# VectorE makes the first sum of two blocks by heads, GpSimd two more steps of each unit, and work at the end of the attention moves ahead of the last stage

## The reference

```
h = layernorm(x) * (1 + ca) + sa
c_kv = h @ W_kv_down;  k = c_kv @ W_k_up;  v = c_kv @ W_v_up;  q = h @ W_q         # 16 heads of 32
q_rope, k_rope = rotary(h @ W_q_rope), rotary(c_kv @ W_k_rope)                      # 32 columns, one for all heads
scores = (q k^T + q_rope k_rope^T) / 8, causal;  w = softmax(scores)
x = x + ga * ((w @ v) @ W_o)
h = layernorm(x) * (1 + cb) + sb
xr, xk = mixes of h with h one token earlier (mu_r, mu_k)
x = x + gb * sigmoid(xr @ W_r^T) * (relu(xk @ W_k^T)^2 @ W_v^T)
```

## Time and profile before

| | |
|---|---|
| time, median of 3 runs | 3523.52 us (3522.85 to 3524.01) |
| the profiled execution | 3526.95 us |
| its span, first to last instruction | 3524.8 us |
| granted TensorE clock, mean | 0.994 |
| PE busy | 3450.0 us, 98% |
| POOL busy | 2799.4 us, 79% |
| DVE busy | 2556.9 us, 73% |
| ACT busy | 1802.9 us, 51% |

### The profile page before, as it was taken

The page is one execution under the profiler, slowest core; times in us unless marked ns, Lnnn a source line. Parts: engine busy times, 40 slices in busy tenths (PEclk is TensorE's granted clock), DMA queues, the critical chain, the costliest instruction groups (busy, mean ns, idle before and its releaser), DMA issues. The chain is left out here.

```text
span 3524.8 us, 53405 instructions
## 1 busy us (share of the span) xinstructions
PE 3450.0 (98%) x19088; PEld 2395.2 (68%) x19088; DVE 2556.9 (73%) x5361; ACT 1802.9 (51%) x3423; POOL 2799.4 (79%) x1252
## 2 busy tenths in 40 slices
PE   8999989999999999999999999999999799999999
PEld 4777756666666666666666666666665588888887
DVE  6777777787877878778778787787775466666665
ACT  2333335556556565565555655656556444344343
POOL 2333359999999999999999999999999566666665
PEclk9999999999999999999999999999999899999999
DMA  5789763463544635526346354363461221111120
GB/s 208 272 285 320 263 165 84 106 152 72 128 106 96 145 80 117 135 70 153 87 111 145 78 124 112 87 155 80 108 154 48 75 72 65 68 68 64 72 72 36
DMA packets 232753, 426.52 MB, mean 121 GB/s; under 512 B 25380, under 2 KB 26916, under 8 KB 232488
## 3 DMA queue, kind: packets, MB, share of 16 engines
q1 hardware_dynamic: 232424, 423.10, 44.6%
q10 hardware_dynamic: 64, 0.02, 0.0%
HBM read 300.86 MB, written 121.65 MB: 120 GB/s over the span
## 5 line engine op out<-in xcount | busy, mean ns | idle before, releaser
L1170 POOL TENSOR_TENSOR att_sum_g<-att_sum_g,att_probs 128x2048 f32<-128x2048 f32 (+3 forms) x458 | 1757.5, 3837 | 53.8 <-ACT att_probs L1070 3.8
L1070 ACT ACTIVATE att_probs<-att_ps_s 128x512 f32<-128x512 f32 (+3 forms) x2560 | 1309.6, 535 | 924.3 <-PE att_ps_s L1231 828.1
L1106 DVE TENSOR_REDUCE att_piece_max<-att_ps_m 128x1 f32<-128x512 f32 x1520 | 964.1, 681 | 242.7 <-PE att_ps_m L1214 240.4
L1230 PE MATMUL att_ps_s<-att_q_a,att_k_a 128*128 128x512 f32 (+3 forms) x2560 | 946.1, 374 | 9.8 <-DMA att_k_b<-s_kr_hi 8.3
L1231 PE MATMUL att_ps_s<-att_q_b,att_k_b 65*128 65x512 f32 (+3 forms) x2560 | 931.3, 368 | 0.0
L1109 DVE CUSTOM_DVE_ANT_0 att_ps_m<-att_ps_m,mask_qk 128x128 f32<-128x128 f32 x1008 | 478.3, 511 | 238.4 <-PE att_ps_m L1214 218.8
L1214 PE MATMUL att_ps_m<-att_k_a,att_q_a 128*128 128x512 f32 (+3 forms) x1808 | 644.1, 380 | 1.5 <-DVE att_piece_max L1106 1.0
L1230 PEld LDWEIGHTS att_ps_s<-att_q_a,att_k_a 128*128 128x128 f32 x2560 | 485.5, 190 | 116.2 <-issue 25.7
L1237 PE MATMUL att_ps_o<-att_probs,att_v 128*32 128x512 f32 (+3 forms) x5120 | 540.1, 534 | 0.0
L1231 PEld LDWEIGHTS att_ps_s<-att_q_b,att_k_b 65*128 65x128 f32 x2560 | 484.0, 189 | 64.9
L1214 PEld LDWEIGHTS att_ps_m<-att_k_a,att_q_a 128*128 128x128 f32 x1808 | 340.1, 190 | 236.9 <-DVE att_piece_max L1106 89.7
(11 more groups left out here) (190 smaller groups left out, 4888.2 us busy)
## 6 DMA issues: line engine op xcount, KB each, us to landing
att_q_a<-s_q_hi SPq DMA_DIRECT2D x128, 256.0 KB, 6.1
att_q_a<-s_qr_hi SPq DMA_DIRECT2D x128, 256.0 KB, 6.8
prj_x_sb<-in_x_dram SPq DMA_DIRECT2D x16, 1024.0 KB, 5.8
s_q_hi<-prj_q_hi SPq DMA_DIRECT2D x16, 1024.0 KB, 4.2
s_q_lo<-prj_q_lo SPq DMA_DIRECT2D x16, 1024.0 KB, 5.4
s_k_hi<-prj_k_hi SPq DMA_DIRECT2D x16, 1024.0 KB, 4.6
s_k_lo<-prj_k_lo SPq DMA_DIRECT2D x16, 1024.0 KB, 7.1
s_v<-prj_v_sb SPq DMA_DIRECT2D x16, 1024.0 KB, 9.0
```

Of the source, the lines that this page charges most:

```text
L1070: act.activation(probs[t % RING][:, hh, c0:CH], ps_s[(GH * t + hh) % SBANKS][:, c0:CH], ACT.Exp, scale=SCALE).then_inc(probs_ready, 1)
L1106: dve.tensor_reduce(top, ps_m[:, bank, :], AX_X, ALU.max).then_inc(piece_taken, 1)
L1170: pool.tensor_tensor(sum_g[:, :, c0:CH], sum_g[:, :, c0:CH], new, ALU.add).then_inc(sum_added, 1)
L1230: mm(out[:, c0:CH], k_a[:, hh, i * P:(i + 1) * P], q_a[j][:, hh, c0:CH], start=True, stop=False)
```

## The change

Five edits in one diff:

1. `SHARE_OF` gives the full steps 8 of block 2 and 6 of block 3 (steps 20 and 30 of a unit) to POOL in place of PE. Block 3 now has no "T" but in the last unit (`SHARE_LAST` is as it was), so whether a block's `ps_d` is opened by the sum is asked for each unit and block.
2. For blocks 2 and 3 DVE makes the first sum, step 0 + step 1, into `sum_g`: four additions of 128x512, one for each head (`open_sum`), in its list for t = FIRST[j] + 3, between parts of that step's maxima. POOL's first add of such a block is now the third step's, and waits for all four (`sum_opened`). ACT waits for `sum_opened` where it reuses the two buffers that DVE reads.
3. `CLOSE_LATER` of block 3 becomes 2 (in the last unit the closing stays at the last t).
4. `deal` counts `OPENING` = 11 in the pairs of steps where DVE opens a sum, and with `CLOSE_LATER` the pair that holds block 3's closing is the one after.
5. The seam: ACT's splits of `w_o` and of the first attention block, DVE's and POOL's low halves of them, PE's turning of `w_r` and ACT's copy of it stand at the end of the attention's lists; the tensors lie over attention buffers no longer in use. SP doesn't wait for the last store at the end of the attention; before it issues that store it waits for all earlier ones, and the last stage waits for it ahead of the load of the second attention block. The first output product waits for all low halves at once.

```diff
-SHARE_OF = ("GGGG", "GGGGGGGG", "GGGGGGGGTGGT", "GGGGGGTGGGGGGGGG")
+SHARE_OF = ("GGGG", "GGGGGGGG", "GGGGGGGGGGGT", "GGGGGGGGGGGGGGGG")
+OPENED_BY_VECTOR = (2, 3)
...
-CLOSE_LATER = (0, 2, 2, 0)
+CLOSE_LATER = (0, 2, 2, 2)
 CLOSES_FIRST = [owners[-1] == "T" and not later for owners, later in zip(SHARE_OF, CLOSE_LATER)]
-OPENED_BY_SUM = ["T" not in (owners.rstrip("T") if first else owners) for owners, first in zip(SHARE_OF, CLOSES_FIRST)]
...
+def opened_by_sum(u, j):
+
+    owners = owners_of(u, j)
+    return "T" not in (owners.rstrip("T") if CLOSES_FIRST[j] else owners)
...
+            if j in OPENED_BY_VECTOR and n < 2:
+                continue
             if n:
...
-PIECE, CLOSING = 2.8, 19
+PIECE, CLOSING, OPENING = 2.8, 19, 11
 
 
 def deal(items, pairs, late, early):
 
-    closes = lambda m: CLOSING * any((FIRST[j] + STEPS[j] + 2 + CLOSE_LATER[j]) % NSTEP == 2 * m for j in range(TCH))
+    closes = lambda m: CLOSING * any((FIRST[j] + STEPS[j] + 2 + CLOSE_LATER[j]) % NSTEP == 2 * m for j in range(TCH)) + \
+        OPENING * any(FIRST[j] + 2 == 2 * m for j in OPENED_BY_VECTOR)
...
+def last_stage_views(nc):
+
+    with ExitStack() as ctx:
+        sb = lambda n, s, d: ctx.enter_context(nc.sbuf_tensor("ffn_" + n, s, d))
+        sb("under_att", [P, 2 * GH * CH + GH * T], F32)
+        att = sb("att_hi", [P, NG, CH], F32R), sb("att_lo", [P, NG, CH], F32R)
+        return att, ctx.enter_context(nc.psum_tensor("ffn_ps_t2", [P, NC, CH], F32))
+
+
+def output_weight(ops):
+
+    return [ops["k_a"][:, part, :].rearrange("p (c n) -> p c n", c=NC) for part in (0, 1)]
...
+        def opened(u, j):
+
+            return GH * (len(OPENED_BY_VECTOR) * u + OPENED_BY_VECTOR.index(j) + 1)
...
-        CLOSE_AT = {t + CLOSE_LATER[j]: (u, j) for t, (u, j) in TAKE_AT.items()}
+        CLOSE_AT = {min(t + CLOSE_LATER[j], NU * NSTEP + LAG - 1): (u, j) for t, (u, j) in TAKE_AT.items()}
...
+            sp.wait_ge(o_stored, 16 * (NU * TCH - 1))
             store_o(NU - 1, TCH - 1)
-            sp.wait_ge(o_stored, 16 * NU * TCH)
...
-                        if owner(t - RING) != "T":
-                            act.wait_ge(sum_added, summed(*STEP_OF[t - RING]))
+                        before = STEP_OF[t - RING]
+                        if before[1] in OPENED_BY_VECTOR and before[2] < 2:
+                            act.wait_ge(sum_opened, opened(*before[:2]))
+                        elif owner(t - RING) != "T":
+                            act.wait_ge(sum_added, summed(*before))
...
+            def split_first():
+                act.wait_ge(ops["w_in"][0], 16)
+                for g in range(NC):
+                    act.copy(output_weight(ops)[0][:, g, :], ops["raw"]["w_o"][:, g, :]).then_inc(ops["wo_hi"], 1)
+                act.wait_ge(ops["att_in"], 16)
+                for g in range(NG):
+                    act.copy(ops["att"][0][:, g, :], ops["raw"]["att"][:, g, :]).then_inc(ops["att_hi"], 1)
...
+                if t == NU * NSTEP:
+                    split_first()
...
+            act.wait_ge(ops["w_turned"], NC)
+            act.copy(receptance_weight(ops)[0], ops["ps_t"][:]).then_inc(ops["w_hi"], 1)
...
+            def open_sum(u, j, hh):
+                s = FIRST[j]
+                if hh == 0:
+                    waits(dve, (probs_ready, heads_ready(u, s + 1, GH - 1)), (closed, TCH * u + j))
+                dve.tensor_tensor(sums[j % 2][:, hh, :], probs[s % RING][:, hh, :], probs[(s + 1) % RING][:, hh, :],
+                                  ALU.add).then_inc(sum_opened, 1)
+
             extras = {t: [] for t in range(NU * NSTEP + LAG + 2)}
+            for u in range(NU):
+                for j in OPENED_BY_VECTOR:
+                    for hh in range(GH):
+                        extras[NSTEP * u + FIRST[j] + 3].append(lambda u=u, j=j, hh=hh: open_sum(u, j, hh))
...
+            def output_weight_low(c):
+                high, low = output_weight(ops)
+                dve.wait_ge(ops["wo_hi"], c + 1)
+                dve.tensor_tensor(low[:, c, :], ops["raw"]["w_o"][:, c, :], as_f32(high[:, c, :]),
+                                  ALU.subtract).then_inc(ops["wo_lo"], 1)
+
             for t, extra in extras.items():
+                if t == NU * NSTEP + LAG:
+                    for c in range(NC):
+                        output_weight_low(c)
...
-                    pool.wait_ge(sum_added, summed(u, j, i) - 1)
+                    if j in OPENED_BY_VECTOR and i == mine[2]:
+                        pool.wait_ge(sum_opened, opened(u, j))
+                    else:
+                        pool.wait_ge(sum_added, summed(u, j, i) - 1)
...
-                        if what == "add" and i in mine[1:]:
+                        if what == "add" and i in mine[2 if j in OPENED_BY_VECTOR else 1:]:
...
+            pool.wait_ge(closed, TCH * (NU - 1) + TCH)
+            for g in range(NG):
+                pool.wait_ge(ops["att_hi"], g + 1)
+                pool.tensor_tensor(ops["att"][1][:, g, :], ops["raw"]["att"][:, g, :], as_f32(ops["att"][0][:, g, :]),
+                                   ALU.subtract).then_inc(ops["att_lo"], 1)
...
+            pe.wait_ge(ops["w_in"][1], 16)
+            pe.wait_ge(probs_ready, heads_ready(NU - 1, NSTEP - 1, GH - 1))
+            for c in range(NC):
+                if c == NC - 1:
+                    pe.wait_ge(o_copied, TCH * NU + 1)
+                for m in range(NC):
+                    last = pe.transpose(ops["ps_t"][:, c, m * P:(m + 1) * P], ops["raw"]["w_r"][:, m, c * P:(c + 1) * P],
+                                        keep["ident_f"][:])
+                last.then_inc(ops["w_turned"], 1)
...
+            sp.wait_ge(ops["o_stored"], 16 * NU * TCH)
             sp.dma_start(att_f[:], att_v[1]).then_inc(att_in, 16)
...
-            act.wait_ge(w_in[0], 16)
-            act.wait_ge(att_in, 16)
-            for g in range(NG):
-                act.copy(att[0][:, g, :], first_att[:, g, :]).then_inc(att_hi, 1)
-                act.copy(w_o[0][:, g, :], w_raw[0][:, g, :]).then_inc(wo_hi, 1)
-            act.wait_ge(att_lo, NG)
-            for i, w in enumerate((w_r, w_k, w_v)):
+            for i, w in ((1, w_k), (2, w_v)):
...
-                if reuse:
-                    pe.wait_ge(att_lo, NG * n + NG)
+                pe.wait_ge(att_lo, NG * n + NG)
+                if not reuse:
+                    pe.wait_ge(ops["wo_lo"], NC)
                 for m in part:
                     if reuse:
                         pe.wait_ge(*bank_free(f"o{m}", n - 1))
                     for c in range(NG):
-                        if not reuse and m == 0:
-                            pe.wait_ge(att_lo, c + 1)
-                            pe.wait_ge(wo_lo, c + 1)
                         last = three_pass(mm, ps[:, m, :], [a[:, c, m * P:(m + 1) * P] for a in att],
...
-            turn_weight(1)
             attention_out(0, False, range(0, 2))
```

More of the change, by code:

```diff
@@ L821, in late_operands, with receptance_weight @@
     ops["att_in"] = ctx.enter_context(nc.semaphore("ffn_att_in"))
+    for name in ("w_turned", "w_hi", "w_lo", "wo_hi", "wo_lo", "att_hi", "att_lo", "o_stored"):
+        ops[name] = ctx.enter_context(nc.semaphore("ffn_" + name))
+def last_stage_views(nc):
[6 more added lines that the diff above has]
+    return [ops["k_a"][:, part, :].rearrange("p (c n) -> p c n", c=NC) for part in (0, 1)]
+def receptance_weight(ops):
+    return [ops["k_a"][:, part, :].rearrange("p (c n) -> p c n", c=NC) for part in (2, 3)]
 def operand_loads(sp, scratch, ops, k_b=None, kb_in=None):
@@ L890, in attention @@
         sum_added = sem("sum_added")
+        sum_opened = sem("sum_opened")
         o_copied = sem("o_copied")
@@ L895, in attention @@
         o_ready = sem("o_ready")
-        o_stored = sem("o_stored")
+        o_stored = ops["o_stored"]
         piece_ready, piece_taken, max_ready = (ops[n] for n in ("piece_ready", "piece_taken", "max_ready"))
@@ L1257, in weighted_values @@
                 if owners_of(u, j)[i] == "T":
-                    first = not OPENED_BY_SUM[j] and i == owners_of(u, j).index("T")
+                    first = not opened_by_sum(u, j) and i == owners_of(u, j).index("T")
                     if first:
@@ L1264, in close_denominators @@
             def close_denominators(u, j):
-                opens = OPENED_BY_SUM[j]
+                opens = opened_by_sum(u, j)
                 if opens:
@@ L1300, in feedforward @@
         pair = lambda n, s: (sb(n + "_hi", s, F32R), sb(n + "_lo", s, F32R))
-        w_o, w_r = ([ops["k_a"][:, k, :].rearrange("p (c n) -> p c n", c=NC) for k in two] for two in ((0, 1), (2, 3)))
+        w_o, w_r = output_weight(ops), receptance_weight(ops)
         w_k = ops["k_next"], sb("w_k_lo", [P, NC, D], F32R)
@@ L1305, in feedforward @@
         att_f = sb("att_f", [P, NG, CH], F32)
-        att = pair("att", [P, NG, CH])
+        sb("att_room", [P, 2 * NG, CH], F32)
+        att = ops["att"]
```

(21 more changed lines are left out.)

## The result

The changed kernel takes 3743.47 us (median of four runs) against 3523.77 for the kernel before beside it: 1.062 times as long, interval 1.061 to 1.064. That is 220 us slower where I forecast 72, and lies outside my range. The profiled execution took 3745.99 us, its span 3744.0.

The account below looks back on a forecast made before the run. PE and POOL were both taken as nearly full. Four pieces made a unit of 147.9 us against 142.9; fifteen loops of +5.0 plus a 3.8 stall gave +79, the tail -7, net +72: 3596 us, range 3540 to 3640.

Parts of the forecast that it names:

- Piece 4: Last part of the unit's loop, from step 43's exponentials to the end of the next j=2 opening: 43.1 us.
- the ring: Five exp buffers: exponentials of step s+5 wait for POOL's add of step s; 4.6 us of slack at step 43.
- The check by POOL alone: Cross-check of the unit: 141.5 us of POOL work, plus idle 4 at one opening and 3 at the other.
- Piece 2: From the end of step 20's add to the end of j=3's opening: 9.5 us, bounds 8.5 and 10.4.
- Pieces 1 and 3: POOL from j=2's opening to step 20's add, 35.1 us, and from j=3's opening to step 38's add, 60.2.
- PE's two products fewer: Ones-products of steps 20 and 30 leave PE, 0.86 us a unit, which buy nothing where POOL sets the time.
- The later closing: j=3 closed two steps later: takes away PE's 1.1 us wait a unit, costs 0.3 at the next closing.
- The tail: Seam between attention and last stage: first output group earlier, -7.4 us, bounds -5 and -9.
- Rival A: Openings of j=2 and j=3 are hidden, the unit is POOL's 141.5 us, the kernel faster at 3496; chance 0.18.
- Rival B: DVE and POOL can't read at once, each head sum costs a POOL add: 60 us in all, 3656; chance 0.15.

Follow-up runs that it names:

- e2: Changed kernel with POOL's clears of steps 36 to 39 one or two adds earlier; 3725.53 us.
- e13: Changed kernel with only POOL's clear of step 37 one add earlier; 3730.81 us.
- e6: Kernel before plus the moved seam and block 3's closing two steps later, old shares, no DVE openings; 3527.65 us, ratio 1.001.
- e7: Changed kernel without DVE's openings: POOL makes the first sums again and keeps steps 20 and 30; 3685.15 us.
- e4: Changed kernel, but PE keeps steps 20 and 30; 3562.31 us, ratio 1.011.
- e5: Kernel before with the moved seam alone; shares, openings and closings as before; 3516.78 us, ratio 0.998.
- e9: Changed kernel with PE keeping steps 20 and 30 and block 3's closing as before, openings at first+3; 3583.27 us.
- e3: Changed kernel with DVE's head sums one step earlier and the clears of steps 36 to 39 one or two adds earlier; 3662.64 us.
- e8: Changed kernel with PE keeping steps 20 and 30 and block 3's closing as before, openings at first+2; 3538.9 us, ratio 1.004.

## Why the forecast was wrong in size

*Piece 4 failed*, "Exponentials of step 43 to the end of the next opening", 43.1. It measured 49.5. The loop does not close at the exponentials of step 43, which nothing holds, but at PE's wait for POOL's clear of step 37. I let POOL be 4.6 us late at the ring before anything stood, and did not follow POOL's list on from the add of step 38, nor PE's queue back to t=39. PE needs POOL's clear of 37 with 0.55 us of slack and block 0's sum with 1.3. e2 and e13 take away the first of these ties and gain only 1.2 and 1.4 us a unit; the later ones stand right behind, as e13's rows show. No run took them all away, so the whole of the 3.3 us is read from rows. The half clock after the stalls (1.65 us in this leg) was not in the sum. Its share is read from rows and from e13's leg; no kernel stalled as long at full clock, so it wasn't isolated. The check by POOL alone in the prediction could have warned me: POOL itself takes 1526.1-(1627.4-142.9) = 41.6 us from the add of step 38 to the end of block 1, so 43.1 leaves it 1.5 of idle time at the opening of j=2, not the 4 that I wrote. It measured 7.8.

*Piece 2 was mis-sized*: 12.2 us for 9.5, above my bound of 10.4. I followed POOL and ACT from the add of step 20; but PE had stood meanwhile (2.92 us), its stretch there ran at a clock of 0.86 (1667.2 to 1679.6), and the exponentials of step 26 began only at 1672.39, 5 us after the release of step 25.

*Pieces 1 and 3 were exact*, 35.1 and 60.2: POOL's time for a full step (4.7) added to its distances in the trace of before.

*The rest of the mechanism was right.* POOL idles in front of both openings, 27 waits; POOL's load is unchanged; and PE's two products fewer don't shorten the unit. I had priced these at half: a step's product is eight matmuls, two groups of four at 0.43 us, so the 16 fewer are 1.7 us a unit and not 0.86. Undone one by one, the new shares cost most: 10.2 us a unit without the openings (e6 to e7), 12.1 with them (e4 to the changed kernel). The openings cost 2.1 with the old shares and 4.0 with the new.

*The later closing* was a gain of 1.1 less 0.3 in my sum. Alone it loses 0.7 a unit (e5, e6): ACT waits where PE had. With the openings at first+3 and the old shares it gains 1.3 (e9, e4).

*The tail* was right: 7.9 us gained (e5) for 7.4.

*Rival A* (hidden openings) didn't happen in any version: POOL idled 4 us or more at an opening even at first+2 with the old shares. *Rival B* (each head sum costs a POOL add) is not what happened here: in the changed kernel the head sums take

```profile
L1179 DVE TENSOR_TENSOR att_sum_g<-att_probs x128: 679/683/2860, 525.2 to 2934.2; 128x512 f32<-128x512 f32 x128
```

at the median the price of one alone. Where the two do meet, the rows show one waiting for the other. In e3 POOL's adds run to 1637.77, and the head started at 1636.01 ends 0.55 us later, the next takes 0.68:

```profile
1636.01 2.31 DVE L1179 TENSOR_TENSOR att_sum_g<-att_probs 128x512 f32<-128x512 f32 x1
...
1638.72 0.68 DVE L1179 TENSOR_TENSOR att_sum_g<-att_probs 128x512 f32<-128x512 f32 x1
```

```profile
1627.02 10.75 POOL L1243 TENSOR_TENSOR att_sum_g<-att_sum_g,att_probs 128x2048 f32<-128x2048 f32 x3
```

That is what the Trainium skill ("SBUF — State Buffer", section "Who interferes with whom") states, and the trace agrees, 2.31 us for 0.68; but such meetings are rare, since POOL mostly idles when the heads come: 2 of the 128 head sums took over 1 us in the changed kernel, 14 in e3.

*Still open*: why e8, with its closing in place and openings at first+2, loses 1.3 us a unit against e5; and how piece 4 divides exactly between clock and waits. For e8 there is a trail in the waits. PE's weight loads for the pieces of the maxima wait for DVE 143.7 us in its 13.9 units and 104.9 in e5's 14, 10.3 a unit for 7.5, so DVE's head sums may cost PE through the maxima. No run isolates it.

## What to carry over

Where two engines are both within 2 us of full in a loop of 143, list every hand-over between them with its slack, those in queue order too (clears, closings), before pricing a delay: the smallest slack counts, which here was not that of the buffer ring, and behind the first tie others can stand nearly as close. Here, handing a step of one to the other cost its full time (4.7 us) and more (7.9). Work taken off an engine is no gain if the engine then starts by waiting for a third. After a stall, count the waiter's clock.
